# A two-layer perceiver: fewer boundary blocks, query stores with semaphores of their own, moved loads, and idle products on TensorE

## The reference

```python
x = x + L0_xattn(layernorm(x), ctx_1024, bias-free mask)     # 16 heads of 16, keys from 1024 context rows
x = x + L0_attn(layernorm(x))      # attention over the 16 positions of dim 0, rope, causal, softmax with 1 + sum
x = x + L0_ffn(layernorm(x))       # router, top 2 of the experts, capacity, gelu, weighted sum, + bias
x = x + L1_xattn(layernorm(x), ctx_1024, bias, padding)
x = x + L1_attn(layernorm(x))      # attention over the 64 queries of a batch, rope, output product
x = x + L1_ffn(layernorm(x))       # gated ffn, inputs and weights rounded to fp4 in blocks of 16
```

## Time and profile before

| what | value |
| --- | --- |
| median of 3 runs | 1383.9 us (1383.46 to 1386.98) |
| profiled execution | 1382.8 us, span 1381.0 us |
| busy | PE 1237.6 us (90%), DVE 970.1 (70%), ACT 785.2 (57%), POOL 634.7 (46%) |
[...]

### The profile page before, as it was taken

The page is one execution under the profiler, slowest core; times in us unless marked ns, Lnnn a source line. Parts: engine busy times, 40 slices in busy tenths (PEclk is TensorE's granted clock), DMA queues, the critical chain, the costliest instruction groups (busy, mean ns, idle before and its releaser), DMA issues. The chain is left out here.

```text
span 1381.0 us, 35067 instructions
## 1 busy us (share of the span) xinstructions
PE 1237.6 (90%) x12294; PEld 1040.4 (75%) x12294; DVE 970.1 (70%) x1995; ACT 785.2 (57%) x1435; POOL 634.7 (46%) x580
## 2 busy tenths in 40 slices
PE   5999999999999689439998899999999999777788
PEld 4788888888888458339985788888888888446455
DVE  5777777777777576457516777777777777578896
ACT  3677777777776211114544577777777777224121
POOL 3656656656654214032332556656656655325000
PEclk9999999999999785559998999999999999887999
DMA  7786776776765120444637686776776765100000
GB/s 214 200 215 177 180 207 175 186 201 175 190 164 137 45 54 3 143 137 151 221 108 219 163 215 178 181 206 176 183 203 176 188 169 131 36 0 3 0 8 24
DMA packets 106725, 198.33 MB, mean 144 GB/s; under 512 B 43661, under 2 KB 63790, under 8 KB 106640
## 3 DMA queue, kind: packets, MB, share of 16 engines
q1 hardware_dynamic: 105104, 193.32, 52.7%
q0 software_dynamic: 1536, 3.88, 0.8%
HBM read 88.26 MB, written 10.62 MB: 72 GB/s over the span
## 5 line engine op out<-in xcount | busy, mean ns | idle before, releaser
L893 POOL TENSOR_SCALAR cross_prob<-cross_prob,cross_inverse 128x1024 f32<-128x1024 f32 x256 | 287.6, 1123 | 335.8 <-DVE cross_inverse L627 335.8
L824 ACT ACTIVATE cross_prob<-cross_negated,cross_negmax 128x1024 f32<-128x1024 f32 x256 | 295.0, 1152 | 136.8 <-DVE cross_negmax L619 136.4
L619 DVE CUSTOM_DVE_ANT_0 cross_negated<-cross_scores,cross_bias 128x1024 f32<-128x1024 f32 x256 | 313.5, 1225 | 28.5 <-PE cross_scores L493 9.9
L506 PE MATMUL cross_turn<-ident,cross_prob 128*128 128x128 f32 x2048 | 268.9, 274 | 8.7 <-ACT cross_probT L833 4.7
L506 PEld LDWEIGHTS cross_turn<-ident,cross_prob 128*128 128x128 f32 x2048 | 239.3, 141 | 49.0 <-POOL cross_prob L893 7.8
L833 ACT COPY cross_probT<-cross_turn 128x512 f32<-128x512 f32 x256 | 149.4, 584 | 64.2 <-PE cross_turn L506 63.2
L635 DVE COPY cross_probT<-cross_turn 128x512 f32<-128x512 f32 x256 | 175.5, 685 | 0.0
L493 PE MATMUL cross_scores<-cross_keys,cross_qbd 96*128 96x512 f32 x512 | 171.0, 415 | 2.7 <-POOL cross_qbd L885 2.7
L873 POOL TENSOR_TENSOR cross_ctx_lo<-cross_raw,cross_ctx_hi 128x512 fp32r<-128x512 f32 x120 | 154.7, 1291 | 12.8 <-DVE cross_probT L695 8.3
L436 PE MATMUL cross_out<-cross_wv_hi,cross_ctx_lo 128*128 128x256 f32 x488 | 148.0, 303 | 0.0
L438 PE MATMUL cross_out<-cross_wv_hi,cross_ctx_hi 128*128 128x256 f32 x488 | 137.9, 283 | 0.0
(11 more groups left out here) (283 smaller groups left out, 2121.3 us busy)
## 6 DMA issues: line engine op xcount, KB each, us to landing
cross_keys<-cross_key_hi SPq DMA_DIRECT2D x512, 128.0 KB, 2.3
cross_raw<-in_ctxT SPq DMA_DIRECT2D x32, 1024.0 KB, 5.5
cross_keys<-cross_key_lo SPq DMA_DIRECT2D x256, 128.0 KB, 2.4
cross_bias<-bias_rows SPq DMA_DIRECT2D x32, 512.0 KB, 3.7
up_sb<-in_moe_w SPq DMA_DIRECT2D x8, 1024.0 KB, 9.1
down_sb<-in_moe_w SPq DMA_DIRECT2D x8, 1024.0 KB, 11.8
cross_stacked_q<-q_rows SPq DMA_DIRECT2D x90, 64.0 KB, 2.0
q_rows<-cross_negated SPq DMA_DIRECT2D x8, 256.0 KB, 2.3
```

Source lines behind the costliest of these rows:

```text
L506: last = pe.transpose(ps_t[part][:, k * P:(k + 1) * P], prob[n % 2][:, kt * P:(kt + 1) * P], ident)
L619: dve.tensor_tensor_reduce(negated[n % 2], ps_s[n % 2][:, :], bias_sb[par][:, :], -1.0, 3.0e38, ALU.add, ALU.min, negmax[:, n % 2:n % 2 + ...
L824: act.activation(prob[n % 2][:, :], negated[n % 2], ACT.Exp, bias=negmax[:, n % 2:n % 2 + 1], scale=-1.0, accum_out=total[:, n % 2:n % 2 + ...
L893: pool.tensor_scalar(prob[n % 2][:, :], prob[n % 2][:, :], inverse[:, n % 2:n % 2 + 1], 1.0, ALU.mult, ALU.mult).then_inc(prob_ready, 1)
```

## The change

- `recycle_semaphores` and its six blocks are gone. `clear_semaphores` issues the same kind of clears on POOL inside other stages: at the start of POOL's list in a cross block, in the project blocks, in `add_turned_block`, and in the experts block behind the first three gathers.
- The four stores of jobs 2 and 3 have a semaphore each; piece p of batch 1's values waits for store p alone. In cross1 the store of job 2 moves ahead of the keys of pairs 5 and 6; in cross0 the order is as it was.
- Of the eight loads of the experts' results, those of j = 2 and 3 move to the start of cross1's list on SP, ahead of the bias and the context.
- `keep_clock` issues fp32 products of the identity with itself, 128x512 unless said, into a bank that nobody reads: two before the last turn of both rope blocks; two at the start of both self attentions; in self attention 0 one for each i below 8 behind scores(i + 1), and one of 256 columns behind weigh for i = 3 to 7; in self attention 1 two each for i = 0 to 2; in the experts block ten of 256 columns at the start and one of 256 behind each of the 17 fp4 turns.

```diff
...
+def clear_semaphores(nc, pool):
+    used = sorted(set(nc.free_semaphores) & set(nc.released_uncleared_semaphores))
+    first = 0
+    for i in range(1, len(used) + 1):
+        if i == len(used) or used[i] != used[i - 1] + 1:
+            pool.sem_clear(range(used[first], used[i - 1] + 1))
+            first = i
+def keep_clock(pe, ident, bank, count=1, columns=512):
+    for _ in range(count):
+        pe.matmul(bank[:, 0:columns].rearrange("p (a n) -> p a n", n=P), ident,
+                  ident.unsqueeze(1).to_broadcast([P, columns // P, P]), start=True, stop=True)
...
             sp.dma_start(t[:, :], self.w[k]).then_inc(self.rows_loaded, 16)
+    def load_taken(self, sp, results, j, loaded):
+        for k in range(2):
+            sp.dma_start(self.home[k][:, 2 * j:2 * j + 2, :],
+                         results.rearrange("(k j i p) d -> k j p i d", k=2, i=2, p=P)[k, j]).then_inc(loaded, 16)
...
         first_q_stored, first_q_loaded = ([sem(f"first_q_{n}{g}") for g in range(G)] for n in ("stored", "loaded"))
-        q_stored, stacked_q_loaded = sem("q_stored"), sem("stacked_q_loaded")
+        q_stored, stacked_q_loaded = [sem(f"q_stored{n}") for n in range(2 * G)], sem("stacked_q_loaded")
...
                 sp.wait_ge(q_step, 3 * n + 3)
-                sp.dma_start(q_rows[0, g * P:(g + 1) * P, at], q_hi(g, c)).then_inc(stored, 16)
-                sp.dma_start(q_rows[1, g * P:(g + 1) * P, at], q_lo(g, c)).then_inc(stored, 16)
+                sp.dma_start(q_rows[0, g * P:(g + 1) * P, at], q_hi(g, c)).then_inc(stored[0], 16)
+                sp.dma_start(q_rows[1, g * P:(g + 1) * P, at], q_lo(g, c)).then_inc(stored[1], 16)
...
                 sp.wait_ge(rows_stored, 32)
+            if taken is not None:
+                for j in range(NT // 4, NT // 2):
+                    first.load_taken(sp, taken["results"], j, taken["loaded"][j])
...
                 first_keys(n)
-            store_queries(0, first_q_stored[0])
+            store_queries(0, [first_q_stored[0]] * 2)
...
             first_queries(0)
-            store_queries(1, first_q_stored[1])
+            store_queries(1, [first_q_stored[1]] * 2)
...
             load_queries(1)
+            store_queries(2, q_stored[0:2])
+            first_keys(4 if taken is None else 5)
             if taken is not None:
-                first_keys(5)
                 first_keys(6)
-            store_queries(2, q_stored)
-            if taken is None:
-                first_keys(4)
-            store_queries(3, q_stored)
+            store_queries(3, q_stored[2:4])
...
             first.load_out(sp)
-            sp.wait_ge(q_stored, 32 * (len(q_jobs) - G))
+            for stored in q_stored:
+                sp.wait_ge(stored, 16)
...
                 act.wait_ge(value_ready, 4 * b + piece + 1)
-                if isinstance(b, int) and b == 1 and piece == 0:
-                    act.wait_ge(q_stored, 32 * (len(q_jobs) - G))
+                if isinstance(b, int) and b == 1:
+                    act.wait_ge(q_stored[piece], 16)
...
+            clear_semaphores(nc, pool)
...
+        @block.gpsimd
+        def _(pool):
+            clear_semaphores(nc, pool)
...
         cleared = sem("cleared")
+        idle_bank = ctx.enter_context(nc.psum_tensor(f"{tag}_idle", [P, 512], F32))
...
                     turn(i - 1)
+            keep_clock(pe, ident, idle_bank, 2)
...
             score_banks = [psum(f"s{a}", [P, BANK]) for a in range(2)]
+            idle_bank = psum("idle", [P, BANK])
...
             ps_t, ps_o = psum("t", [P, blocks, P]), psum("o", [P, units, BANK])
+            idle_bank = ps_o[:, 0, :]
...
+            keep_clock(pe, ident, idle_bank, 2)
...
                     scores(i + 1)
+                if by_position and i < NT:
+                    keep_clock(pe, ident, idle_bank)
+                elif not by_position and i < 3:
+                    keep_clock(pe, ident, idle_bank, 2)
...
                     weigh(i - 3)
+                    if by_position and i < NT:
+                        keep_clock(pe, ident, idle_bank, 1, 256)
...
             sp.wait_ge(loaded, 16 * len(loads))
+        @block.gpsimd
+        def _(pool):
+            clear_semaphores(nc, pool)
...
                 sp.wait_ge(scattered[e], 16 * CT)
-            for j in range(NT // 2):
-                for k in range(2):
-                    sp.dma_start(first.home[k][:, 2 * j:2 * j + 2, :],
-                                 results.rearrange("(k j i p) d -> k j p i d", k=2, i=2, p=P)[k, j]).then_inc(taken_loaded[j], 16)
+            for j in range(NT // 4):
+                first.load_taken(sp, results, j, taken_loaded[j])
...
+            keep_clock(pe, ident, ps_y[0], 10, CAPACITY)
...
                     fp4.turn_tail(pe, n - fp4.ROWS, ps_w[n % 2], ident).then_inc(fp4_turned, 1)
+                keep_clock(pe, ident, ps_h[0], 1, CAPACITY)
...
                 gather(e)
+            clear_semaphores(nc, pool)
...
-def recycle_semaphores(nc):
-    used = sorted(nc.released_uncleared_semaphores)
-    with nc.Block() as block:
-        @block.gpsimd
-        def _(pool):
-            first = 0
-            for i in range(1, len(used) + 1):
-                if i == len(used) or used[i] != used[i - 1] + 1:
-                    pool.sem_clear(range(used[first], used[i - 1] + 1))
-                    first = i
...
             cross_block(nc, f"cross{n}", first, bias_rows[n], dram(f"q_rows{n}", [2, D, T]), x, half_mask, eye, oT, moments, start, taken)
-            recycle_semaphores(nc)
...
                            quarter_mask, half_mask, eye, oT, ahead)
-                recycle_semaphores(nc)
...
                   | {"rows_out": bias_rows})
-        recycle_semaphores(nc)
...
             experts(lambda loads: add_turned_block(nc, "self0_add", oT, eye, x, moments, loads), first, result)
-            recycle_semaphores(nc)
-            cross(1, first, taken={"loaded": taken_loaded, "weight": weight})
+            cross(1, first, taken={"results": results, "loaded": taken_loaded, "weight": weight})
```

## The result

The changed kernel takes 1377.6 us (median of 5 runs, 1372.2 to 1379.3) against 1383.9 (five runs of the kernel before beside it, 1382.6 to 1387.0); the ratio is 0.9946, interval 0.9924 to 0.9969. The forecast was 1379 with a fall of the clock in self attention 0. The profiled execution took 1375.9, span 1374.1. These are the page's first lines; PE is busy 21.8 us longer than the 1237.6 of before, in a span 6.9 shorter.

What follows compares the result with a forecast made beforehand. PE is busy most of the span, but the edited stages are bound in other ways, with PE the bound in self attention 0's loop. −5.8 − 5.5 − 0.8 + 7.1 + 0 = −5.0 us gives 1379, range 1376 to 1382.

Steps and rivals of the forecast that it cites:

- forecast +7.1: Self attention 0's loop: idle products are paid if the clock stays at half, +7.1 us, bounds +6.4 and +7.8.
- The price of an idle product: Four 128x512 products take 1.88 us at full clock, so one costs 0.43 to 0.47, about 0.9 at half.
- the loop's term: Self attention 0: 6.5 us of idle products before scores(7) and 0.86 before the turn behind, +7.1 at half clock.
- It falls as before, and stays: Self attention 0: the clock falls to half despite the few idle products and does not return; forecast's chance 0.55.
- Clears: Six recycle blocks gone from the stage boundaries: −5.8 us, bounds −5.3 and −6.3, with the moved clears hidden on POOL.
- Stores: Job 2's store goes out earlier, ending ACT's stall: 4.9 us in cross1, −5.5 with cross0, bounds −4.2 and −6.3.
- The half microsecond for cross0: Splitting the store semaphore also gains about half a microsecond in cross0, whose own stall was guessed.
- Store 3: In cross1 it keeps its time behind the slipped keys and has landed at 772, for value pieces 2 and 3.
- Loads: Four of eight results loads move from the experts block to cross1: −0.8 us, bounds 0 and −1.1.
- Self attention 1: Idle products fit in waits of 2.69 us or give back their delay: 0, bounds −1.5 and +1.
- The experts' opening: PE waits for gathers there, so the idle products are hidden at either clock.
- the rival "held": Clock held at full in both self attentions: −12.1 − 8 − 4.7 = −24.8 us, 1359; chance 0.15.

## Why the prediction came out right, and what was off

The time (1377.6 for 1379) and the sign were right, and the main reason too: three parts gain, and the loop's idle products give a good part back because the clock is at half where they are paid (0.50 from 515 to 551). But that the idle products' net came out near the forecast +7.1 (9.2 us by the medians of the kernels with and without them, 6.8 by the ratios) is luck. In the profile after it is made of five pieces, of which the forecast had one, at about half its size: the loop +12.8, the opening of self attention 0 −2.4, the fp4 turns +3.2, the experts' opening −2.0 and self attention 1 −3.1. Together they are +8.5. Each is the difference of two single profiles.

- *The price of an idle product was half of what it is.* I divided 1.88 us by four products, but that row counts instructions. The code makes two products there (k in range(G)), and the earlier trace rows show the same: 256 instructions for four score groups of 32 products. One product is two instructions: 0.98 to 1.12 us at full clock, 2.07 at half. That PE is the bound of the loop is in the earlier trace rows, 18.00 and 17.66 of 18.00 us busy at 0.50. By that price the loop's term would have been 14.2 and not 7.1, and the forecast 1386, outside its own range of 1376 to 1382. Measured: 12.8 in the profile after beside the same kernel without them, 7.9 in the kernel with the loop's only. The same price stands in self attention 1, where two products were to take 1.7 us and fit in the 2.69 us wait: at a clock that was partly at half (0.77 over 1236 to 1239) they took 3.07, and did not fit.
- *"It falls as before, and stays" was half right.* It fell at 514 in place of 509.6 (0.81 over 509 to 510 before), which the products in the lead-in gave (worth 2.4 us, forecast at nothing), and came back inside the loop, at 551 in the profile after and at 538 in two others. This saves part of the double price. With no idle product it was at 0.50 until behind the stage; with two a step it fell too, but was back within 4 us and at 1.00 until 555. My judgement named the amount ("but few") as the reason. Between one and two products a step the runs bear it out; what in the products counts, they don't tell apart.
- *Clears:* −5.8 in the gaps, as forecast. *Stores:* −5.9 in cross1 for −4.9, the mechanism as described, no new wait. The half microsecond for cross0 was a guess; its wait of 1.59 us is gone, but a gain there is not resolved. Store 3 did not keep its time but went out about 1 us later (775.23, where the old one, moved with DVE's steps, would be at 774.2), and was still early enough. No run separates the moved order from the four semaphores. *Loads:* the term of −0.8 was sized without the products behind the turns, which I put at some tenths; they cost 3.2, and in the changed kernel the last copy and not a load ends the block. The loads alone gave −1.2. So this pair of edits was a loss of about 2, for a forecast of −0.8.
- *Self attention 1:* 0 was forecast, its stage was 3.1 shorter in the profile after than in the kernel without idle products, and 0.3 to 1.6 shorter in the five others that have its products (boundaries taken off). It is shorter in all six, so the sign is likely real, but the size is the luck of when the clock fell. *The experts' opening* was costed at nothing; it gives 0.6 to 2.0.
- *Rope stages:* −4 us of the difference between the two profiles is in stages that hold no edit but two hidden products. Windows of their beginnings, before and after: the same products at 0.50 and at 1.00.

```profile
478.00:482.00 4.00, 3.80 (x5) 1.76 (x6) 0.00 (x0) 0.00 (x0) 0.00 (x0) 0.50 0.20 46
1202.00:1206.00 4.00, 4.00 (x6) 1.84 (x7) 0.00 (x0) 0.00 (x0) 3.46 (x2) 0.51 0.00 0
```

```profile
478.50:482.50 4.00, 3.85 (x11) 2.20 (x12) 0.99 (x3) 0.00 (x0) 0.00 (x0) 1.00 0.23 44
1201.50:1205.50 4.00, 4.00 (x12) 2.21 (x13) 1.25 (x2) 0.43 (x2) 3.37 (x2) 1.00 0.00 0
```

This does not follow the edits. In the kernel with the clears alone rope 0 took 31.7 again, and in the one with products only around self attention 1 it took 29.6. By windows of 1 us the clock came back there at 482.3 before and 476.5 after, at 483.4 with the clears alone, at 477.1 with products only around self attention 1 and at 482.4 without idle products, and these last two kernels are the same up to there. So it seems to come back a few microseconds earlier or later from one execution to another. That this is a part of why a kernel's runs are spread over 3 to 14 us is likely, but not shown: each kernel has one profile. One profile against another misleads by that much.

For the rival "held" it spoke that the idle products lie in both gaps of the lead-in. These gaps were filled, to 0.64 and 0.93 us of idle time where 3.00 us stood before scores(0), and the clock fell all the same, at 514 with PE 3.00 of 3.00 us busy. So filled gaps were not enough here.

Five kernels have the three other parts and none of the loop's products. Four of them are the best ones: 1367.4 to 1369.1, below both the kernel before and the changed one. The fifth, with the 17 behind the turns only, took 1371.8. Which of the other idle products are worth having is not resolved between them.

## What to carry to other kernels

Instructions whose only use was to keep the clock up cost 5.5 to 12.8 us here in a loop that their engine bounds, and each had about twice its price (2.07 us for 1.12 or less) where the clock was at half all the same: put them where the engine waits anyway, and keep them out of loops in which the engine has no idle time. Before pricing an instruction from a row with a count, compare the count with the loop in the code. Where one semaphore covers several transfers, look which of them the waiter needs: here an order and four semaphores were worth as much as six barriers (7.7 and 7.4 us by the medians, each alone).

## What the runs showed of the hardware

- An fp32 product appears as two instructions on PE in these traces: the 32 score products of a tile are x64, and the two idle products before scores(0) are x4 with 1.96 us.
- PE that was 100% busy, mostly on small tiles, neither kept nor raised its clock here: it was busy for 3.00 of 3.00 us when the clock fell at 514, and for 12.00 of 12.00 at 0.50 in the kernel without the loop's products. With two products of 128x512 in a step of the same loop the granted clock was 1.00 over 518 to 548, with one it was 0.50 there.
